# Delta rule: the keys' causal convolution after the projection, on ScalarE and GpSimd, in place of four tap-weighted projections

## The reference

```python
def _causal_dw_conv_silu(x, w):          # 4 taps, one set per channel
    ... # y[t] = sum_j w[:, j] * x[t - 3 + j]
    return jax.nn.silu(y)
q = l2norm(_causal_dw_conv_silu(x @ Wq, conv_q).reshape(b, t, 8, 128))
k = l2norm(_causal_dw_conv_silu(x @ Wk, conv_k).reshape(b, t, 8, 128))
v = _causal_dw_conv_silu(x @ Wv, conv_v).reshape(b, t, 8, 32)
# per head: state = a * (state - beta * (state k) k^T) + beta * v k^T;  out = state q
```

## Time and profile before

| | |
|---|---|
| three runs | 4041.48, 4056.18, 4058.17 us (median 4056.18) |
| profiled execution, span from first to last instruction | 4054.5 us |
| PE busy (matmul) | 3480.2 us, 86% |
| VectorE busy | 2420.3 us, 60% |
| ScalarE busy | 1593.8 us, 39% |
| GpSimd busy | 537.6 us, 13% |
| mean granted TensorE clock | 0.869 |

### The profile page before, as it was taken

One profiled execution on the slowest core, in us unless ns is written; L12 is line 12 of the kernel. 1 busy time (PEld: TensorE's weight loads), 2 busy tenths in 40 slices (PEclk: granted clock), 3 DMA queues, 4 the chain that ended last, 5 costly groups with the idle time before them and its releaser, 6 DMA issues. The chain is left out here.

```text
span 4054.5 us, 124079 instructions
## 1 busy us (share of the span) xinstructions
PE 3480.2 (86%) x55256; PEld 2205.5 (54%) x55256; DVE 2420.3 (60%) x6248; ACT 1593.8 (39%) x2941; POOL 537.6 (13%) x564
## 2 busy tenths in 40 slices
PE   3877777679999998899977796999999999999985
PEld 1326665225555555555556342666666666666672
DVE  3757776337777667767775112566666666666545
ACT  1653333345444444444320243444434344443323
POOL 1212222000000000000000000222222222222210
PEclk9896667789888888989765797999999999999967
DMA  2000000121111111111000001000000000000000
GB/s 88 0 0 1 1 1 1 43 72 51 47 39 36 41 36 44 41 44 34 13 3 3 16 0 44 2 3 3 3 2 2 3 3 3 3 3 3 2 3 23
DMA packets 37030, 77.12 MB, mean 19 GB/s; under 512 B 7696, under 2 KB 11153, under 8 KB 35473
## 3 DMA queue, kind: packets, MB, share of 16 engines
q1 hardware_dynamic: 36496, 69.17, 5.3%
HBM read 64.83 MB, written 4.33 MB: 17 GB/s over the span
## 5 line engine op out<-in xcount | busy, mean ns | idle before, releaser
L1366 PE MATMUL ps<-g_hs,g_fc 128*128 128x512 f32 x448 | 276.0, 701 | 40.9 <-ACT g_hidden L1488 22.0
L1488 ACT ACTIVATE g_hidden<-ps 128x512 f32<-128x512 f32 x224 | 133.3, 595 | 383.9 <-PE ps L1366 383.3
L2133 PE MATMUL ps<-d_hp,d_w_k 128*128 128x512 f32 x512 | 282.5, 638 | 0.0
L1257 PEld LDWEIGHTS ps<-g_Q,g_K 32*32 32x32 f32 x12288 | 193.8, 114 | 144.9 <-issue 57.3
L2211 POOL TENSOR_TENSOR d_sq<-d_QK 128x512 f32<-128x512 f32 x128 | 133.0, 1039 | 934.0 <-ACT d_QK L2262 772.7
L1257 PE MATMUL ps<-g_Q,g_K 32*32 32x32 f32 (+1 forms) x12288 | 225.1, 218 | 34.4 <-issue 10.1
L1380 PE MATMUL ps<-g_hidden,g_proj 128*128 128x512 f32 x448 | 243.0, 636 | 0.0
L2231 ACT ACTIVATE d_F<-ps 128x128 f32<-128x128 f32 x256 | 70.8, 276 | 352.9 <-PE ps L2042 349.6
L1225 POOL COPY g_xb<-X 128x512 f32<-128x512 f32 x8 | 7.3, 907 | 1232.4 <-DVE X L1686 1121.5
L2406 DVE SCALAR_TENSOR_TENSOR d_conv<-ps,w_conv_q,d_conv 128x511 f32<-128x511 f32 (+2 forms) x192 | 142.3, 741 | 34.2 <-ACT d_conv L2256 30.3
L1366 PEld LDWEIGHTS ps<-g_hs,g_fc 128*128 128x128 f32 x448 | 79.5, 210 | 149.1 <-ACT g_hidden L1488 80.5
(11 more groups left out here) (479 smaller groups left out, 7885.7 us busy)
## 6 DMA issues: line engine op xcount, KB each, us to landing
g_hs<-gate_rows SPq DMA_DIRECT2D x56, 256.0 KB, 3.6
g_fc<-in_c_fc_dram SPq DMA_DIRECT2D x56, 256.0 KB, 4.1
g_proj<-in_c_proj_dram SPq DMA_DIRECT2D x56, 256.0 KB, 2.8
X<-in_x_dram SPq DMA_DIRECT2D x1, 2048.0 KB, 11.0
w_c_fc<-in_c_fc_dram SPq DMA_DIRECT2D x1, 2048.0 KB, 8.0
w_c_proj<-in_c_proj_dram SPq DMA_DIRECT2D x1, 2048.0 KB, 12.4
ex_root<-gate_rows SPq DMA_DIRECT2D x1, 2048.0 KB, 15.0
h_rows<-k SPq DMA_DIRECT2D x1, 2048.0 KB, 6.3
```

Source lines behind the costliest of these rows:

```text
L1257: ins = e.matmul(later(scored, n_), keys_, queries(n_, planes, r_, 4 * i + j), start=(turn_ == 0 and part == 0 and n_ != 1), stop=(part == 1),
L1366: e.matmul(P[2], fc[:, n % 2, ts(f, C)], hs[:, n % 2], start=True, stop=True).then_inc(pe.steps, pe.did(now(f"u{i}")))
L1488: e.activation(r[:, slot], P[2], ACT.Relu).then_inc(act.steps, act.did(now(f"r{i}")))
L2133: ins = e.matmul(b, w_k[:, j, ts(H, C)], hp_of(u)[:, j:j + T], start=(j == 0), stop=(j == TAPS - 1))
```

## The change

The tap-weighted key weights go. `Wqk3` (plain query and key weights, 1 MB) and `conv_k` are loaded with the layer's other constants, and the two blocks' loads, the copy of the query weights and the four multiplications on VectorE go with them.

A key head is projected once, at turn 8, place 0. ScalarE then copies it four times out of PSUM, each time scaled by one tap, into four rows of a new tile `ktaps`: two copies at turn 8, two at turn 0 (place 2). GpSimd adds the shifted rows 1, 2 and 3 into row 0, at turns 1, 2 and 3. ScalarE's silu of the key head reads `ktaps` row 0 and moves from turn 3 to turn 4; the summing of the key squares on PE moves from turn 5 to turn 6. PSUM bank 5 is free again when the four copies are read.

```diff
-        w_q, w_k = k.sb("d_w_q", [C, 8 * C], stack=s), k.sb("d_w_k", [C, TAPS, 8 * C], stack=s)
+        w_q, w_k = k.w["Wqk3"][:, 0], k.w["Wqk3"][:, 1]
+        ktaps = k.sb("d_key_taps", [C, TAPS, T], stack=s)
...
-            @block.sync
-            def _(e):
-                e.dma_start(w_plain, k.dram["Wqk3"]).then_inc(dma.steps, dma.did("plain"))
-                e.wait_ge(dma.steps, dma.at("plain"))
...
-        for n in (1,):
-            pe, act, dve, pool, dma = k.stage(f"delta_taps{n}")
...
-                    e.dma_start(taps, src.to_broadcast([C, TAPS, 8 * C])).then_inc(dma.steps, dma.did("taps"))
...
-                    e.tensor_copy(w_q[:], w_plain[:, 0]).then_inc(dve.steps, dve.did())
-                    e.wait_ge(dma.steps, dma.at("taps"))
-                    for j in range(TAPS):
-                        e.tensor_tensor(w_k[:, j], w_plain[:, n], taps[:, j], ALU.mult).then_inc(dve.steps, dve.did())
...
-                    elif x % 8 >= 4:
-                        put(u, turn, "taps", x, place={8: 0, 0: 0, 1: 1}.get(turn % NI, 2))
+                    elif x % 8 == 4:
+                        put(u, turn, "taps", x, place=0)
+                        for y in range(2):
+                            put(u, turn + y, "kscale", 2 * (x // 8) + y)
+                        for late in range(1, TAPS):
+                            put(u, turn + 1 + late, "kadd", TAPS * (x // 8) + late)
...
-                    put(u, NI * (x // 2) - 46 + 4 * (x % 2), "taps_done", x, place=(1 if x % 2 == 0 else 2))
-                    put(u, NI * (x // 2) - 42 + 2 * (x % 2), "squares", x)
+                    put(u, NI * (x // 2) - 46 + 5 * (x % 2), "taps_done", x, place=(1 if x % 2 == 0 else 2))
+                    put(u, NI * (x // 2) - 42 + 3 * (x % 2), "squares", x)
...
-                            ins = e.matmul(b, w_k[:, j, ts(H, C)], hp_of(u)[:, j:j + T], start=(j == 0), stop=(j == TAPS - 1))
+                            e.matmul(b, w_k[:, ts(H, C)], hp_of(u)[:, 3:3 + T], start=True, stop=True).then_inc(pe.steps, pe.did(f"{tag}run{run}"))
...
+                        elif what == "kadd":
+                            h, late = x // TAPS, x % TAPS
+                            if late == 1:
+                                e.wait_ge(act.steps, act.at(f"{tag}kread{h}"))
+                            else:
+                                e.wait_ge(pool.steps, pool.at(f"{tag}kadd{x - 1}"))
+                            e.tensor_tensor(ktaps[:, 0, late:], ktaps[:, 0, late:], ktaps[:, late, 0:T - late], ALU.add).then_inc(pool.steps, pool.did(f"{tag}kadd{x}"))
...
+                        elif what == "kscale":
+                            h = x // 2
+                            if x % 2 == 0:
+                                e.wait_ge(pe.steps, pe.at(f"{tag}run{2 * h + 1}"))
+                                if u or h:
+                                    e.wait_ge(act.steps, act.at(f"{tag}run{2 * h - 1}" if h else f"u{u - 1}run7"))
+                            for late in (2 * (x % 2), 2 * (x % 2) + 1):
+                                e.activation(ktaps[:, late], tap_bank(1), ACT.Copy, scale=k.w["conv_k"][:, 4 * g + h, 3 - late:4 - late]).then_inc(act.steps, act.did(f"{tag}kread{h}"))
...
-                                e.wait_ge(pe.steps, pe.at(f"{tag}run{x}"))
-                            e.activation(QK[:, x % 2, 4 * (u % 3) + x // 2], cv if x % 2 == 0 else tap_bank(x), ACT.Silu).then_inc(act.steps, act.did(f"{tag}run{x}"))
+                                e.wait_ge(pool.steps, pool.at(f"{tag}kadd{TAPS * (x // 2) + 3}"))
+                            e.activation(QK[:, x % 2, 4 * (u % 3) + x // 2], cv if x % 2 == 0 else ktaps[:, 0], ACT.Silu).then_inc(act.steps, act.did(f"{tag}run{x}"))
```

More of the change, by code:

```diff
@@ L123 @@
     "gla": ["W_in2", "b_in2", "W_qka", "b_qka", "W_v2", "b_v2", "W_y2", "b_y2", "W_out2", "b_out2", "h0", "gla_mask"],
-    "delta": ["conv_q", "Wv3", "Wg3", "Wab3", "Wo3", "A_log", "dt_bias", "conv_v", "o_norm_w", "joins", "eye32", "upto3", "ones3", "picks"],
+    "delta": ["conv_q", "conv_k", "Wqk3", "Wv3", "Wg3", "Wab3", "Wo3", "A_log", "dt_bias", "conv_v", "o_norm_w", "joins", "eye32", "upto3", "ones3", "picks"],
     "mix": ["W_r3", "W_k3", "W_v3", "mu"],
@@ L1865, in delta_rule @@
         pe, act, dve, pool, dma = k.stage("delta_start")
-        w_plain = QK[:].rearrange("p c h t -> p (c h t)")[:, 20 * T:].rearrange("p (c f) -> p c f", c=2)
         with nc.Block() as block:
-            @block.sync
-            def _(e):
-                e.dma_start(w_plain, k.dram["Wqk3"]).then_inc(dma.steps, dma.did("plain"))
-                e.wait_ge(dma.steps, dma.at("plain"))
             @block.scalar
@@ L1884, in delta_rule @@
         k.end()
-        taps = QK[:].rearrange("p c h t -> p (c h t)")[:, 0:TAPS * 8 * C].rearrange("p (j f) -> p j f", j=TAPS)
-        for n in (1,):
-            pe, act, dve, pool, dma = k.stage(f"delta_taps{n}")
[L1888 to L1891, removed]
-                    e.dma_start(taps, src.to_broadcast([C, TAPS, 8 * C])).then_inc(dma.steps, dma.did("taps"))
-                @block.vector
-                def _(e):
-                    e.tensor_copy(w_q[:], w_plain[:, 0]).then_inc(dve.steps, dve.did())
-                    e.wait_ge(dma.steps, dma.at("taps"))
-                    for j in range(TAPS):
-                        e.tensor_tensor(w_k[:, j], w_plain[:, n], taps[:, j], ALU.mult).then_inc(dve.steps, dve.did())
-            k.end()
         f2 = lambda ap: ap.rearrange("p h t -> p (h t)")
@@ L2130, in prepare @@
                                 return
-                            if j == 0 and (u or run > 1):
-                                e.wait_ge(act.steps, act.at(f"{tag}run{run - 2}" if run > 1 else f"u{u - 1}run{run + 6}"))
-                            ins = e.matmul(b, w_k[:, j, ts(H, C)], hp_of(u)[:, j:j + T], start=(j == 0), stop=(j == TAPS - 1))
-                            if j == TAPS - 1:
-                                ins.then_inc(pe.steps, pe.did(f"{tag}run{run}"))
+                            if u or run > 1:
+                                e.wait_ge(act.steps, act.at(f"{tag}kread{run // 2 - 1}" if run > 1 else f"u{u - 1}kread3"))
+                            e.matmul(b, w_k[:, ts(H, C)], hp_of(u)[:, 3:3 + T], start=True, stop=True).then_inc(pe.steps, pe.did(f"{tag}run{run}"))
                         elif what == "squares":
@@ L2728, in layouts @@
     o["conv_q"] = c(i["L3_attn_conv_q"].reshape(8, C, 4).transpose(1, 0, 2))
-    o["conv_qk"] = c(np.stack([i["L3_attn_conv_q"].T, i["L3_attn_conv_k"].T], 0))
+    o["conv_k"] = c(i["L3_attn_conv_k"].reshape(8, C, 4).transpose(1, 0, 2))
     o["Wv3"] = c(i["L3_attn_Wv"])
```

## The result

| | before | after |
|---|---|---|
| median of four runs each | 4057.18 us | 4157.82 us |
| ratio of after to before, 95% interval | | 1.0245 (1.022 to 1.027) |
| profiled execution, span | 4054.5 us | 4157.1 us |
| mean granted clock, whole span | 0.869 | 0.818 |
| PE, VectorE, ScalarE, GpSimd busy | 3480.2, 2420.3, 1593.8, 537.6 | 3486.4, 2431.7, 1743.1, 756.0 |

The forecast was 4150 us with a range of 4010 to 4215. 384 key-tap instructions are gone, and yet PE is busy 6 us longer.

A forecast was written before the change was run, and what follows sets the result against it. PE looked like the bound, but waits behind the removed taps would limit the gain. The forecast was 4054.5 - 15.5 (start) + 6 (first heads) - 30 (cycles) + 136 (clock) = 4151, given as 4150 us, range 4010 to 4215.

The forecast's parts named there:

- Start: -15.5: Before PE's first delta-rule matmul: tap-weight loads and multiplications go, saving 15.5 us (bounds -16 and -12).
- First heads: +6: Before the first chunk: copies and additions lengthen five heads from 7.3 to 8.5 us each, +6 us (0 to +10).
- Cycles at full clock: -30: Over 59 steady cycles: removed taps gain only 0.5 us a cycle, -30 us (bounds -12 and -196).
- the three waits: PE's waits at turns 0, 1 and 2, leaving gains of 0.43, 0 and 0.2 us from the removed taps.
- The gain of 0.5: Net gain per steady cycle at full clock from removing three taps: 0.5 us, less for first chunks included.
- Rival B: Steady cycles: PE is the bound and its queue closes over the removed taps, 3843 us; chance 0.05.
- Clock: +136: Steady cycles: TensorE's clock falls for 6 us a cycle, costing 2.3 us each, +136 us (0 to +265).
- the forecast's price: Steady cycles: each us at half clock costs 0.45 us, less about a seventh that falls into PE's waits.
- the state product at about double its time: Expected sign in the steady part: state product at about double its 1.87 us in many cycles.
- the thin stretch: From key projection's end at turn 8 to turn 3's q products: only small PE work without the taps, 9.7 us.
- Rival A: Steady part: TensorE's clock holds, so the kernel takes 4015 us, faster by 1%; chance 0.18.
- Rival C: Turns 1 to 3: GpSimd's additions block VectorE's small SBUF operations, +48 us on Rival A, 4063 us; chance 0.07.

The follow-up runs named there:

- Experiment 2: Kernel before, with only the last of a key head's four taps projected and no copies or additions added: 4126.68 us, ratio 1.0179.
- Experiment 8: Changed kernel with the first unit's key additions on VectorE in place of GpSimd: 4142.56 us, ratio 1.0223.
- Experiment 1: Changed kernel with PE repeating the key projection, unread, at turns 0, 1 and 2: 4075.04 us, ratio 1.005 to the kernel before.
- experiment 3: Changed kernel with all four scaled copies of a key head at turn 8, none at turn 0: 4141.3 us, ratio 1.0198.
- experiment 4: On top of experiment 3, query projection, values and one gate piece moved to earlier turns, no work added: 4274.2 us, ratio 1.055.
- experiment 5: Changed kernel with all four copies at turn 8 and three unread key projections at turns 0, 1 and 2: 4054.0 us, ratio 0.9987.

## Why the prediction was right, and where it was not

**Start: -15.5, measured -15.1 by the start of PE's first matmul, -15.5 by its wait.** PE's wait ahead of its first matmul in the delta rule was 31.41 us and is now:

```profile
2482.84 2.05 PE L2084 MATMUL ps<-X,w_center 128*128 128x512 f32 x2 [15.87 <-PEq L71]
```

In the eight other profiled kernels with the new start this wait is 15.7 to 17.9 us, so the agreement to a tenth is luck and the size is not.

**First heads: +6, measured +17.6. This term was mis-sized**, beyond its own bound of +10. I added up 8.5 us a head; the copies above follow one another at 11.4 to 11.9. What the sum left out stands in PE's queue: the next key projection is behind the matmul of the squares, so GpSimd's squares and that matmul are in the ring too, and the matmuls run at half clock. One turn of it after: copies 2.42, three additions 3.6, silu 0.63, the first of two squares 1.0, the squares' matmul 1.8, the projection 2.1, some 11.6 us in all against the 11.9 from one head's copies to the next's. PE waits 5.94 us in it for GpSimd:

```profile
2527.69 2.04 POOL L2191 TENSOR_TENSOR d_sq<-d_QK 128x512 f32<-128x512 f32 x2 [0.81 <-ACT d_QK L2257]
...
2528.78 1.88 PE L2121 MATMUL ps<-d_sq,w_picks 128*8 128x512 f32 x2 [5.94 <-POOL d_sq L2191]
2530.59 2.07 PE L2115 MATMUL ps<-d_hp,w_Wqk 128*128 128x512 f32 x2
```

Experiment 2 has neither copies nor additions and takes 57.8 us from PE's first matmul to the first chunk, with a clock of 0.77 there; the changed kernel takes 78.0 at 0.71, the kernel before 60.4 at 0.90. So the clock alone does not stretch the first heads. Experiment 8 shows that the additions are in the ring (4.8 us by moving them); how the rest divides was read from the timeline and not tested by itself.

**Cycles at full clock: -30, and the three waits it was built on.** At turn 0 the forecast had PE wait 3053.56 - 3053.03 = 0.53 us for VectorE's output ahead of the state product; it waits 0.52 us on average, in 29 cycles, and in 14 others 0.7 us ahead of the broadcast of g. Turn 1 was forecast with PE idle 1.4 us ahead of f1; the timeline has 1.38 and PE's waits over the cycles name it first:

```profile
PE ps L2055 <- DVE d_O L2383: 15.1, 29, 0.5
PE ps L2024 <- DVE d_X L2330: 61.7, 52, 1.5
PE ps L2024 <- ACT d_F L2218: 25.1, 30, 1.8
```

(13.6 us over 37 times for the same transpose before, and 20.4 over 37 for a later one that PE no longer waits for.) F's copy is late, as forecast, in half of the cycles. The places of the waits were right. The gain of 0.5 itself cannot be seen, since no run has the taps away and the clock up. Rival B (PE the bound all the way, 3843) is out: the idle time grew where its chains said.

**Clock: +136.** The sign and the cause hold: experiments 1 and 2 change only PE's matmuls and move the clock both ways. The time at half clock was put too low: 8.0 us a cycle (0.4 before), not 6. What it costs by itself no run shows, since the clock and the removed work change together. The two terms of the cycle together were forecast at (136 - 30) / 59 = +1.80 us and measured at +1.70. With 7.6 us more at half clock and the forecast's price (0.45, less a seventh) the first would be 2.9 us, and the gain 1.2 in place of 0.5; with the forecast's gain the price would be 0.29. PE's busy time leans to the first reading: the taps took 199.5 / 59 = 3.38 us a cycle out and it still grew by 0.18, so the other work took 3.56 us longer, 0.47 for each us at half clock. Its idle time grew by 1.53, so 1.85 of the 3.38 came back. That the sum came out so close is therefore partly luck: a time at half clock that was too short was made up for by a price that was too high or a gain that was too small. The total within 0.2% of 4157.8 owes something to luck as well: the first heads' miss of +12 us stands against the cycles' miss of -5.

**Where in the cycle it falls: wrong.** I expected the state product at about double its time. Over the 44 chunks that have one, its instructions are the same as before (ns min/median/max; before, then after):

```profile
L2073 PE MATMUL ps<-d_S,d_QK x704: 190/277/419, 2593.1 to 3848.1; 128*128 128x32 f32 x176
```
```profile
L2055 PE MATMUL ps<-d_S,d_QK x704: 192/276/419, 2595.3 to 3951.1; 128*128 128x32 f32 x176
```

In the clock's record it is down at the start of the transpose ahead of f1 in 18 of the 59 cycles, and 3 us later in 56. So it mostly falls at the end of the thin stretch, and what pays most are the q products, the squares and the query projection behind it, with 108 of the 210 us by which the work other than the key projection grew. I had it "about half the thin stretch" and only a part of the query projection.

**Rival A (the clock holds, 4015) and the Trainium skill.** "TensorE: Matmul & The Clock Gate", in its section on oscillation, ties the fall to gaps in which PE idles. Idle gaps did appear (the waits above), none longer than 1.8 us. With one unread projection at turn 1, where the largest of the waits was, that wait falls from 64.9 us (experiment 3) to 8.5, and the clock still is 0.88. So the trace goes against the rule as it reads for gaps: the clock moved with the wide work in the cycle. Whether its amount or its place decides is not shown; experiment 4 kept the amount and changed the places, but brought waits of up to 3.9 us with it.

**Rival C (GpSimd blocks VectorE, 4063).** Experiment 1 has all additions and costs 0.24 us a cycle, and moving the copies out of F's way gives all of that back (experiment 5, 21.80 us). The long operations are there and cost the cycle nothing that shows: the unit's small SBUF operations are long after as before.

```profile
L2415 DVE TENSOR_SCALAR d_t<-d_z x16: 175/869/1133, 2511.2 to 3884.9; 128x16 f32<-128x16 f32 x16
```

## What to carry to other kernels

Before you take matmuls out of PE's queue, ask what clock the rest will run at: find a stretch of the trace where that work already stands alone and read its granted clock, and price the wide instructions that come behind it. Then ask which chain is next in line, since each of the three freed places here had a wait behind it (0.5 to 0.7 us on average at turn 0, 1.2 at turn 1, 0.8 at turn 2, in 43, 52 and 30 of the 59 cycles). In a start-up ring, count all that stands in each engine's queue between two turns of it, not only what the data depend on.

## What the hardware showed that was not expected

- Matmuls that nobody reads made this kernel faster: two a cycle took it from 4141 to 4054 us. PE's busy time went down with them, from 1240.0 to 1207.3 us in the 59 cycles.
- Leaving out three quarters of the key projection made the kernel before slower by 1.8%.
- PE's first matmul of the last stage started between 2475.8 and 2488.6 us in the nine profiled kernels that have the changed start (experiment 2 has the old one), though all that runs before it is the same. Absolute starts of one execution each differ by that much; differences of 5 us have to be read from the phase's own start.
